# Two-block expert layers of a four-layer network: batches of four blocks up and four down, three PSUM pairs, outputs and side products in two banks

## The reference, cut to what matters

```
gate_logits = xf @ Wg + bg
top_w, top_i = top_k(gate_logits, 2); top_w = softmax(top_w)
for e in range(8):
    h = gelu(xf @ W1[e] + b1[e])        # 64 -> 256
    y = h @ W2[e] + b2[e]               # 256 -> 64
    out += gate[:, e:e+1] * y           # gate: top_w where e was chosen, else 0
```

## Time and profile before

| | us |
|---|---|
| median of 3 runs | 2091.02 (2087.83 to 2093.96) |
| profiled execution | 2093.26 |
| its span | 2091.5 |
| PE busy | 1754.5 (84%) |
| DVE busy | 1019.8 (49%) |
| ACT busy | 913.0 (44%) |
| POOL busy | 494.1 (24%) |
| up matmuls L600, all four expert layers | 457.3 busy |
| down matmuls L612 | 435.3 busy |
| gelu L680 | 474.4 busy, 1109 ns each |
| scaling L815 | 190.4 busy, 750 ns each |

### The profile page before, as it was taken

The page is one execution under the profiler, slowest core; times in us unless marked ns, Lnnn a source line. Parts: engine busy times, 40 slices in busy tenths (PEclk is TensorE's granted clock), DMA queues, the critical chain, the costliest instruction groups (busy, mean ns, idle before and its releaser), DMA issues. The chain is left out here.

```text
span 2091.5 us, 52780 instructions
## 1 busy us (share of the span) xinstructions
PE 1754.5 (84%) x21380; PEld 771.8 (37%) x21380; DVE 1019.8 (49%) x1964; ACT 913.0 (44%) x1222; POOL 494.1 (24%) x677
## 2 busy tenths in 40 slices
PE   5877999987998788777688886599999667699997
PEld 2442333333333223233477773233333222233332
DVE  1445675723554466350166663566665167243341
ACT  3123555553444444443344444355555410555553
POOL 0000222220000144300255650023232146022222
PEclk8797999997999899988899997899999889799998
DMA  6001323210000344335533322031313020124333
GB/s 221 11 11 41 73 51 77 46 41 30 11 0 0 83 111 103 70 97 198 196 98 98 126 73 91 0 82 42 81 44 79 0 30 10 46 67 102 82 71 81
DMA packets 62286, 145.09 MB, mean 69 GB/s; under 512 B 35240, under 2 KB 35240, under 8 KB 57984
## 3 DMA queue, kind: packets, MB, share of 16 engines
q1 hardware_dynamic: 62208, 144.14, 25.7%
HBM read 106.09 MB, written 25.44 MB: 63 GB/s over the span
## 5 line engine op out<-in xcount | busy, mean ns | idle before, releaser
L680 ACT ACTIVATE ARENA<-PS,W 128x1024 f32<-128x1024 f32 x448 | 474.4, 1109 | 327.9 <-PE PS L600 327.6
L531 POOL TENSOR_TENSOR ARENA<-ARENA 128x512 f32<-128x512 f32 x224 | 293.0, 1308 | 1254.2 <-DVE ARENA L815 1251.0
L600 PE MATMUL PS<-ARENA,W 64*128 64x512 f32 x1792 | 457.3, 630 | 0.4 <-ACT ARENA L680 0.4
L612 PE MATMUL PS<-ARENA,W 128*64 128x512 f32 x1792 | 435.3, 607 | 14.4 <-DVE ARENA L815 14.4
L815 DVE SCALAR_TENSOR_TENSOR ARENA<-PS,W,ARENA 128x512 f32<-128x512 f32 x256 | 190.4, 750 | 340.4 <-PE PS L612 273.9
L600 PEld LDWEIGHTS PS<-ARENA,W 64*128 64x128 f32 x1792 | 158.4, 191 | 259.7 <-issue 151.3
L612 PEld LDWEIGHTS PS<-ARENA,W 128*64 128x64 f32 x1792 | 109.3, 137 | 304.2 <-issue 207.1
L1192 DVE TENSOR_TENSOR ARENA<-ARENA 128x1024 f32<-128x1024 f32 x64 | 75.6, 1222 | 67.7 <-PE PS L1125 34.5
L1162 ACT ACTIVATE ARENA<-PS 128x1024 f32<-128x1024 f32 x64 | 62.0, 1021 | 91.5 <-PE PS L1115 91.5
L1724 PE MATMUL PS<-ARENA 32*32 32x32 f32 x8448 | 97.1, 195 | 5.5 <-issue 5.4
L1724 PEld LDWEIGHTS PS<-ARENA 32*32 32x32 f32 x8448 | 94.0, 105 | 8.2 <-issue 6.4
(11 more groups left out here) (216 smaller groups left out, 2139.8 us busy)
## 6 DMA issues: line engine op xcount, KB each, us to landing
ARENA<-scratch_g SPq DMA_DIRECT2D x64, 768.0 KB, 9.5
ARENA<-scratch_g SPq DMA_DIRECT2D x64, 256.0 KB, 3.9
W<-w_dram SPq DMA_DIRECT2D x1, 7323.0 KB, 30.1
ARENA<-XN SPq DMA_DIRECT2D x12, 512.0 KB, 3.4
ARENA<-XN SPq DMA_DIRECT2D x16, 256.0 KB, 2.3
scratch_x<-ARENA SPq DMA_DIRECT2D x8, 512.0 KB, 5.6
scratch_b<-ARENA SPq DMA_DIRECT2D x8, 512.0 KB, 4.8
scratch_z<-ARENA SPq DMA_DIRECT2D x8, 512.0 KB, 3.9
```

What stands on the lines that cost most here:

```text
L531: nc.gpsimd.tensor_tensor(SUM[:, k, :], SUM[:, k, :], TMP[:, e % 2, :], ALU.add)\
L600: last = mm(PS[:, (b % 2) * R + r, :], w(layer + "_w1", b * 128, (b + 1) * 128, half(r)), XE[half(r), k, :], start=True, stop=True)
L612: last = mm(PS[half(r), 4 + e % 2, :], w(layer + "_w2", b * C, (b + 1) * C), H[:, b % 4, r * T:(r + 1) * T], start=part == 0, stop=part == ...
L680: f(H[:, b % 4, :], PS[:, (b % 2) * R:(b % 2) * R + R, :].rearrange("p a b -> p (a b)"), ACT.Gelu, bias=w(layer + "_b1", b, b + 1)).then_i ...
```

## The change

A new function `deep_experts` serves L0, L2 and L3; `experts` stays for L1. It computes the same. What differs:

- A batch is four blocks up and four down (`BAT = 4`), so a tile has four batches.
- The ups take three PSUM pairs in turn (`UPS = 3`, banks 0 to 5), and `H` has six slots (`HS = 6`). The up of block u waits for the gelu of block u-3, and the gelu of u for the output of the expert that block u-6 belongs to.
- The outputs and the side products take turns in banks 6 and 7, in the order of the list `order`; each waits until the one before it in its bank has been read (`after_scale` names the expert that must be scaled; other waits are in `emptied`).
- The side products stand at other places, and so do DVE's and ACT's steps (`pe_at`, `act_at`, `dve_at`).
- TensorE and ACT have all 16 tiles written out, with no loop. The copy of the gates lies in `ROWS` instead of the arena.

```diff
+        def deep_experts(layer, norms=1, router=None):
+            BAT, UPS, HS = 4, 3, 6
+            XS, H = a.take(2, T), a.take(HS, R * T)
+            RT = ROWS[:, 0:2 * T].rearrange("p (k t) -> p k t", k=2)
...
+            NBAT = NB // BAT
+            if norms:
+                order = ["center", 0, 1, "vary", 2, 3, "logits", 4, 5, "turn", 6, 7]
+                after_scale = {0: 0, 2: 2, 4: 4, 6: 6, "center": -1, "vary": 1, "logits": 3, "turn": 5}
+                at_last = {3: 1, 5: 3, 7: 5}
+                pe_at = {0: "center", 0.5: "vary", 2: "logits", 3: "turn"}
+                act_at = {(0, 1): "square", (2, 3): "bend", (3, 1): "rows"}
+                dve_at = {-1: "keep", 1: "start 3 3", 2: "3 norm", 3: "rank", 5: "weigh"}
+            else:
+                order = [0, 1, "logits", 2, 3, 4, 5, "turn", 6, 7]
+                after_scale = {0: -1, 1: 0, 2: 2, 4: 3, 5: 4, 6: 6, "logits": 1, "turn": 5}
+                at_last = {7: 5}
+                pe_at = {1: "logits", 3: "turn"}
+                act_at = {(1, 3): "bend", (3, 1): "rows"}
+                dve_at = {1: "rank", 3: "weigh"}
+
+            def out_of(unit):
+                return UPS * R + order.index(unit) % 2
...
+                    def behind(unit, t):
+                        count = t * E + after_scale[unit]
+                        if count > 0:
+                            pe.wait_ge(e_scaled.sem, e_scaled.at(count))
...
+                    def up(u):
+                        t, b = divmod(u, NB)
+                        if norms and b == 0:
+                            pe.wait_ge(ln_normed.sem, ln_normed.at(t + 1))
+                        if u >= UPS:
+                            pe.wait_ge(e_gelu.sem, e_gelu.at(u - UPS + 1))
+                        for r in range(R):
+                            last = mm(PS[:, (u % UPS) * R + r, :], w(layer + "_w1", b * 128, (b + 1) * 128, half(r)),
+                                      XS[half(r), t % 2, :], start=True, stop=True)
+                        last.then_inc(e_hidden.sem, 1)
+
+                    def emptied(t, e):
+                        if t == 0 and e == 1 - norms:
+                            pe.wait_ge(g_rows.sem, g_rows.at(1))
+                        if e in after_scale:
+                            behind(e, t)
+                        elif t == NT - 1:
+                            if e in at_last:
+                                pe.wait_ge(e_scaled.sem, e_scaled.at(t * E + at_last[e]))
+                        elif e == 7:
+                            pe.wait_ge(g_rows.sem, g_rows.at(t + 2))
+                        elif norms and e < 5:
+                            pe.wait_ge(ln_taken.sem, ln_taken.at((t + 1) * 2 + (e + 1) // 2))
+                        else:
+                            pe.wait_ge(g_taken.sem, g_taken.at(t + 2))
...
+                    for t in range(NT):
+                        for n in range(NBAT):
+                            for u in range(t * NB + (n + 1) * BAT, t * NB + (n + 2) * BAT):
+                                if u < NT * NB:
+                                    up(u)
+                            if t + 1 < NT:
+                                prepare(pe_at.get(n), t + 1)
+                            for b in range(n * BAT, (n + 1) * BAT):
+                                down(t, b)
+                            if t + 1 < NT:
+                                prepare(pe_at.get(n + 0.5), t + 1)
...
+                    def bend_up(u):
+                        act.wait_ge(e_hidden.sem, e_hidden.at(u + 1))
+                        if u >= HS:
+                            act.wait_ge(e_out.sem, e_out.at((u - HS) // blocks + 1))
...
-        experts("L0")
+        deep_experts("L0")
...
-        experts("L2")
+        deep_experts("L2")
...
-        experts("L3", norms=0, router=once)
+        deep_experts("L3", norms=0, router=once)
```

More of the change, by code:

```diff
@@ L816, in tile_of @@
                                 TMP[:, e % 2, :] if e else SUM[:, k, :], PS[:, 4 + e % 2, :],
+                                w(layer + "_b2", e, e + 1), WB[:, k, e, :],
+                                ALU.add, ALU.mult).then_inc(e_scaled.sem, 1)
+                            if more:
+                                prepare(dve_at.get(e, ""))
+                        dve.wait_ge(e_added.sem, e_added.at((t + 1) * (E - 1)))
+                        v.tensor_tensor(tile(X, t), tile(X, t), SUM[:, k, :], ALU.add).then_inc(e_fold.sem, 1)
@@ new lines, in _ @@
+                    prepare = prepare_all(0, 0)
+                    for e in sorted(dve_at):
+                        prepare(dve_at[e])
+                    with dve.Fori(0, NT // 2 - 1) as i:
+                        for k in range(2):
+                            tile_of(i * 2 + k, k, i)
+                    tile_of(NT - 2, 0, NT // 2 - 1)
+                    tile_of(NT - 1, 1, NT // 2 - 1, more=False)
+            if not norms:
+                for c in e_input:
+                    c.base += NT // 2 * INPUT
@@ new lines, in experts @@
+            e_hidden.base += NT * NB
+            e_gelu.base += NT * NB
+            for c in e_first + e_rest:
+                c.base += NT // 2 * (R * 16)
+            g_kept.base += NT * 16
+            for c in (e_out, e_scaled):
+                c.base += NT * E
+            e_added.base += NT * (E - 1)
+            e_fold.base += NT
+            for c in (ln_centered, ln_squared, ln_varied, ln_normed):
+                c.base += NT * NORMS
+            ln_taken.base += NT * NORMS * 2
+            ln_newton.base += NT * NORMS * NEWTON
```

238 lines of the change are left out of this document (added).

## The result

| | before | changed |
|---|---|---|
| median | 2091.35 us (4 runs) | 2075.85 us (4 runs, 2067.35 to 2078.41) |
| ratio, 95% interval | | 0.9892 [0.9853, 0.9931] |
| profiled execution, its span | 2093.26, 2091.5 | 2067.35, 2065.6 |
| median in a later comparison | 2093.09 (12 runs) | 2081.47 (7 runs), ratio 0.9931 [0.9905, 0.9957] |

A forecast was written before the change was run, and what follows sets the result against it. TensorE alone was taken to bound the expert stretches. Savings of 8.1 us each in first and third experts and 23.0 in the last sum to 39 us, giving 2052 us; range 2034 to 2067.

The forecast's parts named there:

- With 16 tiles, 4 pairs less each: 64 x 0.36 = 23 us a layer: First, third and last experts: 4 instead of 8 up-down pairs a tile save 23 us a layer, 69 us for three.
- L0: (tiles - 1) x (34.45 - 33.94) + 1.4 - 1: First experts: 15 tiles shorten from 34.45 to 33.94, plus 1.4 for the last tile, less 1 at the start: 8.1 us.
- TensorE alone sets these stretches: First and last experts: TensorE busy 263.98 of 264 and 247.62 of 248 us, ACT only 142 and 135.
- 0.36 us a pair of entries, runs of 3.63 and 3.58: Entering up mode costs 0.21 us, down 0.16; four ups take 3.63, four downs 3.58, a batch 7.21.
- The ring's cover: Fourth up of a batch, with three PSUM pairs: first gelu done at 2.24, needed at 2.68; cover 0.4 us, no wait.
- the slots of H: Third gelu of a batch waits for the first expert's down in the same batch: cost 0, at most 38 us.
- the loops: Straight code replacing loops on TensorE and ACT costs 0 and gains nothing; 21 turns of loops go.
- A new wait of 0.95 us before the turn: First and third experts: two scalings before the weighing delay the turn 0.95 us in each tile preparing another; bounds 0 and 1.6.
- The logits wait 0.05: First and third experts: norm chain ends near 20.1, logits due at 20.17, in time by a hair; 0.05 us put.
- Gates of the next tile, first tiles: Next tile's gates are hidden; in first and third experts' first tile, vary waits for expert 0's scaling, 1 us a layer.
- The clock falls at the new wait: Rival: clock drops at each turn wait, 1.64 us a fall, 30 tiles, 49 us lost, time 2101; chance 0.05.
- The time from one profile of before, less the sum: Whole kernel: profiled 2093.3 us less 39 is 2054; median 2.2 lower than that execution, so 2052.

The follow-up runs named there:

- two experiments: Changed kernel with L3 alone in batches of two blocks, 2089.81 us (ratio 0.9971); and with L3 alone in batches of one block, 2111.65 us.

## Why the prediction was wrong, and where it was right

**The step that failed is the number of tiles: "With 16 tiles, 4 pairs less each: 64 x 0.36 = 23 us a layer".** There are 8, so 32 pairs a layer and 96 in all, not 192; and 14 tiles wait for the turn, not 30. Each price was per batch or per tile, so every total halved. The prediction's own working with 8 tiles:

| term | 16 tiles, as predicted | 8 tiles | measured in the profile |
|---|---|---|---|
| L3, pairs x 0.36 | 23.0 | 11.5 | 13.0 |
| L0: (tiles - 1) x (34.45 - 33.94) + 1.4 - 1 | 8.1 | 4.0 | 4.3 |
| L2, the same | 8.1 | 4.0 | 2.6 |
| sum | 39 | 19.5 | 19.9 |

2091 less 19.5 would have been 2071.5; measured were 2075.85 and 2081.47, so 4 to 10 us of the gain that the experts show are missing from the medians. The agreement of the sums is partly luck: L2 fell short, L3 gained more than its term, and L0 and L2 vary by 1 to 3 us from profile to profile.

Point by point:

- *TensorE alone sets these stretches*: right; its idle in L3 is 0.85 of 240 us.
- *0.36 us a pair of entries, runs of 3.63 and 3.58*: right, and 0.35 by two experiments. (By its own terms it is 7.58 - 7.21 = 0.37.) That up runs pitch like down runs was assumed there, and holds.
- *The ring's cover, the slots of H, the loops*: nothing, right; each was tried by itself. The cover of the ring was the third pair's doing: with two pairs the batch costs 0.78 us more. (Of loop turns 9 went, not 21.)
- *A new wait of 0.95 us before the turn*: right, 0.97, with the sequence and the 4.14 us taken from the earlier trace rows. But it holds in 14 tiles, not in 30.
- *The logits wait 0.05*: too small; 0.16 to 0.27 in ten of the 14 tiles, 0.04 or nothing in the others. The working took the end of the norm chain from the earlier trace rows less two waits. It left out that POOL's add now falls on an early step of the chain, 0.55 to 0.66 instead of 0.43. With the turn's wait gone the tiles are 33.17 to 33.27, so the logits cost 0.21 to 0.31 over 32.96 and the turn 1.02. Hence tiles of 34.19 to 34.29 where 33.94 was forecast: 0.25 to 0.35 us in each of ten tiles, 3 us.
- *Gates of the next tile, first tiles*: charged 1 us in L0 and L2, for `vary` waiting until expert 0 is scaled, and nothing in L3. The wait is in the trace, once in each of the two layers, 0.65 and 0.66 us. From the first tiles' lengths nothing finer can be read: L3's is 27.26 with the change and was 26.30 to 27.65 without it.
- *The last tile*: not thought of. 0.85 us in three layers. The rule that banks take turns was read only for the tiles that prepare another.
- *The clock falls at the new wait*: did not happen; clock 1.00 from 174 to 440 us with about 0.97 us of idle in each tile.
- *The time from one profile of before, less the sum*: sound for the part that changed, but the rest of this kernel is not constant. It was 1058 to 1079 us in the profiles with the change, a spread as large as the whole gain, and the single profile of before could not show that.

The sign did not hang on the count, the size did: with 8 tiles every case among the rivals would have stood at about half its distance from the kernel before, and the range would have been narrower with them.

## What to carry to other kernels

A price per batch is worth only as much as the count it is multiplied by: check the count of trips against a row's xcount (here 384 gelus = 3 x 16 x 8) before the sum, since it scales all terms at once. Alternating row-half and column-half matmuls costs 0.35 us a pair at these shapes, so let each run as long as the PSUM ring, the banks and the side work allow; two ring pairs made it a loss. After such a regrouping, look for what small DVE work now stands behind a scaling or beside a POOL add on its way to the bound engine: moving two steps in a table gave another 16 us in the layers here (12 and 18 by the two medians of the changed kernel), nearly as much as the change itself.

## What the runs showed of the hardware

- The price of going from ups to downs and back is in proportion to how often it is done, from 4 to 16 pairs a tile: 0.353 and 0.352 us a pair (fp32, 512 columns, clock 1.00).
- A DVE step of 0.22 us lasts up to 1.20 when a POOL add of 1.3 us is under way, and one of 0.16 lasts 0.89; both end less than 0.1 us after the add. A scaling with an operand in PSUM lasts 0.74 to 0.75 in either case.
- A stage in which TensorE is busy for 80 to 84% was granted between 0.76 and 0.90 of the clock from run to run (first mixer, same instructions, 112.9 to 126.2 us), while the stretches of the first and last experts shown above had 1.00.
